# One eviction copy for the column transform, and a filter layer that contracts over 64 rows: a whitening, Fourier filter and MLP kernel on Trainium2

## The chip, the cores and the metric

The kernel runs on one core of one Trainium2 chip. The metric is device microseconds (us) of one execution, the median of the runs shown. TensorE (PE) has two entries in the profile, matrix multiplications (PE) and weight loads (PEld); VectorE is DVE, ScalarE is ACT, GpSimd is POOL, and SyncE (SP) issues the transfers.

## What is computed

The input x holds 16 images of 56 x 56 pixels with 64 channels, in fp32. Cut to what matters here:

```
x  = L^-1 (x - mean) * gamma + beta       # L: Cholesky factor of the 64 x 64 channel covariance
h  = layer_norm(x)
xf = rfft2(h)                             # per image, over rows and columns, 29 x 29 kept parts
o1 = relu(w1 * xf + b1)                   # complex, block diagonal: 8 blocks of 8 x 8 channels
o2 = softshrink(w2 * o1 + b2)             # complex, block diagonal
h  = irfft2(o2) + h + x
out = gelu(layer_norm(h) @ mw1 + mb1) @ mw2 + mb2 + h     # 64 -> 256 -> 64 channels
```

## The kernel before

Two images are one pair: its 2 x 56 image rows stand on 112 partitions, and 56 x 64 numbers in each. There are 8 pairs, numbered 0 to 7 here. A first part reads all pairs once for the covariance and factors it. Then every pair goes through whitening, the filter and the MLP in one software pipeline: in the step of pair i, TensorE runs the filter of pair i, and between its pieces the whitening of pair i + 1 and the MLP of pair i - 1. Each engine's order is written out by hand in its own program; a loop covers the middle pairs, and the first and the last steps are written out. Engines meet only through counting semaphores. SP issues the load of a pair behind the seven stores of an earlier one.

The filter of a pair begins with three stages that go through one ring of four PSUM banks (`ring_b`, lines 246 and 247). A chunk may be written once the chunk four places before it has been read out; `free_b` (line 866) waits for that.

- `dft_h` (line 922): 8 chunks of the row transform. ACT evicts each with one copy of 112 x 464 (line 1121).
- `dft_w` (line 934): 8 chunks of the column transform, 4 matmuls each, 1 in the last. The result of a chunk holds image b in partitions 64b to 64b + 63 (32 channels, real and imaginary part of the row transform) and, in the free dimension, the sum over the cosines (s = 0) and over the sines (s = 1). ACT evicts it into `p_y` with four copies of 64 partitions (line 1133): image b's part s goes to partitions 64s to 64s + 63, so that one matmul of 128 rows adds the cosine and the sine part.
- `layer_1` (line 944): 8 chunks, of 435 columns (four times) and of 406, one matmul of 128 rows each with one of two weight sets `w1s`; chunk k is image k % 2. Their results are evicted with bias and relu in two instructions of 64 partitions each: by ACT (line 1142) for chunks 0 to 3, 5 and 7, and by DVE (line 639) for chunks 4 and 6. These move each image's real and imaginary parts from partitions to where the second layer wants them.

Behind `layer_1` TensorE transposes the first slice of the previous pair's normalised tensor (line 1016) and whitens two chunks (line 918), which need earlier whitening chunks evicted by DVE (line 630). Then the MLP's first matmul (line 1030) waits for that transposed slice `n2T`: ACT writes its high part (line 1166), DVE its low part (line 662). ACT does this behind its layer 1 evictions. DVE does it behind the second layer norm of the previous pair (statistics on line 539, small steps on lines 559 to 567 and 415 to 419, lines 580 and 586), two whitening evictions (line 630) and its layer 1 evictions (line 639).

The tables come in with two transfers among the loads of the first part: `cst` (652 KB) and `prm` (771.5 KB). DVE multiplies the weights with their masks there (line 464).

Of the kernel before, what the change touches and what calls it, by code (L numbers as in the profile page):

```python
# [25 lines left out]
ALU = mybir.AluOpType  # L26
# [93 lines left out]
CONST_COLS = {"f1": 2 * KR, "f2": 4 * KF, "invw": 2 * 224, "invh": ROWS, "mask1": 128, "mask2": 128,  # L120
              "below": C, "minus": C, "ident": 128}
PARAM_COLS = {"w1": 256, "w2": 256, "mw1": HID, "mw2": 2 * 128, "beta": C, "g1": C, "b1": C, "mb2": C,
# [11 lines left out]
def build(nc, x, consts, params, out):  # L134
# [5 lines left out]
    with ExitStack() as ctx:  # L140
        def sb(name, shape, dtype=F32):
            return ctx.enter_context(nc.sbuf_tensor(name, shape, dtype))
# [10 lines left out]
        def pp(name, rows=128):  # L153
            return prm[0:rows, p_at[name][0]:p_at[name][1]]
# [3 lines left out]
        w1s = sb("w1s", [128, 256])  # L158
# [60 lines left out]
        DV_WEIGHTS = 7  # L219
# [32 lines left out]
        p_v = p_y[:, 0:2 * 2 * SPEC].rearrange("p (b h k w) -> p b h k w", b=2, h=2, k=KF)  # L252
# [44 lines left out]
        with nc.Block() as block:  # L297
# [114 lines left out]
            def _(dve):  # L412
# [8 lines left out]
                def covariance_and_factor():  # L421
# [40 lines left out]
                    for t, src, mask in ((w1s, "w1", "mask1"), (w2s, "w2", "mask2")):  # L462
                        for h in range(2):
                            link(nc.vector.tensor_tensor(t[:, 128 * h:128 * h + 128],
                                                         pp(src)[:, 128 * h:128 * h + 128], cc(mask), ALU.mult))
# [343 lines left out]
            def _(pe):  # L809
# [300 lines left out]
            def _(act):  # L1110
# [149 lines left out]
def constants():  # L1260
# [35 lines left out]
    m1 = np.zeros((2, 2, CH, 2, 2, CH))  # L1296
    for cs, r in ((0, 0), (0, 1), (1, 0), (1, 1)):
        for s, sign in enumerate((1.0, -1.0)):
            to_re = (cs == r)
            coef = {(0, 0): 1.0, (1, 1): sign, (0, 1): sign, (1, 0): -1.0}[cs, r]  # L1300
            m1[cs, r, :, s, 0] = same * coef * (1.0 if to_re else -1.0)
            m1[cs, r, :, s, 1] = same * coef
# [13 lines left out]
def layout(i):  # L1316
# [16 lines left out]
    a = np.zeros((2, 2, G, BS, 2, 2, 2, G, BS), np.float32)  # L1333
    for cs in range(2):
        for r in range(2):
            for ro in range(2):
                part = ro if cs == r else 1 - ro
                a[cs, r, :, :, :, :, ro] = w1[part].transpose(1, 2, 0, 3)[:, :, :, None, None, :]
# [39 lines left out]
```

## Time and profile before

| | |
|---|---|
| median of 3 runs | 1033.61 us (1033.3 to 1036.7) |
| the profiled execution | 1037.1 us, of which the span of its instructions 1035.2 us |
| mean granted TensorE clock | 0.927 of full |
| PE busy | 908.7 us, 88% |
| DVE busy | 716.5 us, 69% |
| ACT busy | 557.1 us, 54% |

The profile is one execution. Times in the rows below are us from the start of its span. The column transform starts at 194.1 us for pair 0, and then at 269.2, 369.7, 474.0, 577.3, 679.6, 781.5 and 878.5 us for pairs 1 to 7. Fp32 matmuls stand as two instructions each in the trace, so a count there is twice that of the program.

### The profile page before, as it was taken

What the parts mean: (1) busy time and instruction counts of PE and PEld (TensorE: products, weight loads), DVE (VectorE), ACT (ScalarE), POOL (GpSimd) and SP (SyncE); (2) the same over time, 40 slices, a digit from 0 to 9 for tenths busy, and PEclk for the clock granted to TensorE, in tenths of its full rate; (3) what the DMA queues carried; (4) which work ended last, traced back from release to release, by engine and by line L of the source; (5) the groups of instructions that cost most, each with busy time, mean ns of one, the idle gap of its engine ahead of it and who ended that gap; (6) DMA issues with size and microseconds to landing.
All of it is one profiled execution on the core that took longest, in us unless ns stands there. A gap on an engine that the chain in (4) does not pass through costs nothing.

```text
span 1035.2 us, 18451 instructions
## 1 busy us (share of the span) xinstructions
PE 908.7 (88%) x6263; PEld 775.4 (75%) x6263; DVE 716.5 (69%) x2061; ACT 557.1 (54%) x1139; POOL 261.0 (25%) x107
## 2 busy tenths in 40 slices
PE   5888973887999988998899889988998999799687
PEld 5886552765689768976897689768976997499465
DVE  4356779169957876877677777877788688543762
ACT  0002001674777586757675767586748754875333
POOL 2000001333332234223422342234315324330110
PEclk8995556889999999999999999999999999899789
DMA  9950202002000020002000200110000000000001
GB/s 258 233 125 1 62 1 62 2 1 62 2 10 28 28 63 9 27 19 71 9 27 22 68 11 25 33 57 18 18 27 1 20 27 20 0 28 26 11 28 36
DMA packets 9956, 40.78 MB, mean 39 GB/s; under 512 B 1232, under 2 KB 1232, under 8 KB 8208
## 3 DMA queue, kind: packets, MB, share of 16 engines
q1 hardware_dynamic: 9888, 40.00, 14.3%
q8 instruction: 27, 0.44, 0.2%
q14 instruction: 41, 0.34, 0.1%
HBM read 27.15 MB, written 12.85 MB: 39 GB/s over the span
## 4 chain that ended last, share of the span: by engine, by line
PE 53%; DVE 21%; issue 10%; ACT 9%; DMA 6%; DVEq 0%; SPq 0%; ACTq 0%
PE psum L1045 16%; PE psum L1030 8%; PE psum L983 8%; DMA n<-x_dram 6%; ACT p_y L1133 5%; PE psum L964 4%; DVE stats L539 4%; PE psum L930 3%; ACT o_g L1142 3%; PE psum L918 3%; PE psum L1004 3%; PE psum L857 3%; DVE o_g L294 2%; PE psum L905 2%; PE psum L1016 2%
## 5 line engine op out<-in xcount | busy, mean ns | idle before, releaser
L1174 ACT ACTIVATE hid<-psum,hbias 128x448 f32<-128x448 f32 x224 | 136.1, 633 | 141.4 <-PE psum L1030 140.5
L1045 PEld LDWEIGHTS psum<-prm,hid 128*112 128x112 f32 x1792 | 186.2, 182 | 8.5 <-ACT hid L1174 4.5
L1045 PE MATMUL psum<-prm,hid 128*112 128x96 f32 x1792 | 190.5, 266 | 2.2 <-ACT hid L1174 2.2
L364 POOL TENSOR_TENSOR hbuf<-hbuf,prm 112x1792 f32<-112x1792 f32 x15 | 51.6, 3439 | 337.5 <-DVE hbuf L613 337.5
L662 DVE TENSOR_TENSOR n2T<-psum,n2T 64x448 fp32r<-64x448 f32 x112 | 69.7, 622 | 94.4 <-ACT n2T L1166 93.1
L1030 PE MATMUL psum<-n2T,mw1h 128*128 128x448 f32 x224 | 103.3, 461 | 30.0 <-DVE n2T L662 17.4
L392 POOL TENSOR_TENSOR p_y<-over,under 116x512 f32<-116x512 f32 x64 | 77.5, 1212 | 167.1 <-ACT under L1192 167.0
L983 PE MATMUL psum<-cst,p_y 116*128 116x224 f32 (+1 forms) x480 | 101.8, 355 | 3.0 <-POOL p_y L392 3.0
L983 PEld LDWEIGHTS psum<-cst,p_y 116*128 116x128 f32 (+1 forms) x480 | 89.9, 194 | 6.2 <-POOL p_y L392 3.2
L1133 ACT COPY p_y<-psum 64x232 f32<-64x232 f32 (+1 forms) x256 | 84.3, 329 | 13.9 <-PE psum L940 10.3
L1030 PE MATMUL psum<-n2T,mw1l 128*128 128x448 f32 x224 | 84.1, 376 | 0.0
L1030 PEld LDWEIGHTS psum<-n2T,mw1h 128*128 128x128 f32 x224 | 43.8, 195 | 50.2 <-DVE n2T L662 19.2
L371 POOL TENSOR_TENSOR rbuf<-hbuf,ybuf 112x3584 f32<-112x3584 f32 x8 | 62.7, 7835 | 69.8 <-DVE fbuf L699 63.7
L382 POOL TENSOR_TENSOR fbuf<-fbuf,prm 112x3584 f32<-112x3584 f32 x7 | 54.4, 7773 | 101.1 <-DVE n L586 101.1
L1115 ACT ACTIVATE xT<-psum,negm 128x448 f32<-128x448 f32 x56 | 35.5, 636 | 80.6 <-PE psum L905 80.4
L951 PE MATMUL psum<-p_y,w1s 128*128 128x406 f32 (+1 forms) x128 | 60.7, 563 | 20.2 <-ACT o_g L1142 10.9
L539 DVE BATCH_NORM_STATS2 stats<-fbuf 112x6 f32<-112x64 f32 x448 | 58.5, 210 | 28.2 <-issue 28.2
L1121 ACT COPY u_r<-psum 112x464 f32<-112x464 f32 x64 | 34.9, 546 | 74.8 <-PE psum L930 74.8
L930 PE MATMUL psum<-cst,hbuf 112*112 112x116 f32 x512 | 55.3, 271 | 17.1 <-DVE hbuf L798 17.1
L1166 ACT CAST n2T<-psum 64x448 fp32r<-64x448 f32 x112 | 58.8, 525 | 21.3 <-PE psum L1016 19.6
L930 PEld LDWEIGHTS psum<-cst,hbuf 112*112 112x112 f32 x512 | 55.0, 185 | 20.3 <-issue 20.0
L680 DVE TENSOR_TENSOR oslice<-psum,fbuf 112x512 f32<-112x512 f32 x56 | 38.5, 687 | 45.5 <-PE psum L1045 44.5
(114 smaller groups left out, 1714.2 us busy)
## 6 DMA issues: line engine op xcount, KB each, us to landing
xin<-x_dram SPq DMA_DIRECT2D x9, 1568.0 KB, 8.6
out_dram<-oslice SPq DMA_DIRECT2D x56, 224.0 KB, 2.2
ybuf<-x_dram SPq DMA_DIRECT2D x2, 1568.0 KB, 21.5
fbuf<-x_dram SPq DMA_DIRECT2D x2, 1568.0 KB, 25.1
n<-x_dram SPq DMA_DIRECT2D x2, 1568.0 KB, 28.5
xin<-x_dram SPq DMA_DIRECT2D x4, 392.0 KB, 6.0
prm<-params_dram SPq DMA_DIRECT2D x1, 771.5 KB, 29.7
cst<-consts_dram SPq DMA_DIRECT2D x1, 652.0 KB, 21.1
```

Of the source, the lines that this page charges most:

```text
L371: nc.gpsimd.tensor_tensor(r4, h_tok, y4, ALU.add).then_inc(r_ready, 1)
L392: nc.gpsimd.tensor_tensor(yk, a, b, ALU.subtract).then_inc(y_ready, 1)
L539: last = nc.vector.bn_stats(stats[:, w, :], src[:, w * C:(w + 1) * C])
L662: last = nc.vector.tensor_tensor(n2T[C * (1 - v):C * (1 - v) + C, v, :], ring_c[k % RING_C][C * v:C * v + C, 0:4 * ROWS], n2T[C * v:C * v ...
L930: last = nc.tensor.matmul(t[0:ROWS, j * 2 * KR:(j + 1) * 2 * KR], h_w[:, 4 * k + j, :], cc("f1", ROWS), start=True, stop=True)
L951: nc.tensor.matmul(t[:, 0:(z - a) * KF], w1s[:, 128 * half:128 * half + 128], p_v[:, b, half, a:z, :].rearrange("p k w -> p (k w)"), start ...
L983: last = nc.tensor.matmul(t[:, j * 224:j * 224 + n * 112], y_v[0:n * KR, kp, 128 * r:128 * r + 128], inverse(r, n), start=(r == 0), stop=( ...
L1030: last = nc.tensor.matmul(t[:, 0:4 * ROWS], wt[:, HH * m:HH * m + HH], n2T[:, v, :], start=(p == 0), stop=(p == 1))
L1045: last = nc.tensor.matmul(t[0:ROWS, at:at + 96], hid[:, m, w % 2, (w // 2) * ROWS:(w // 2 + 1) * ROWS], pp("mw2")[:, 128 * m + zeros:128 * ...
L1133: last = nc.scalar.copy(p_v[C * s:C * s + C, b, :, 4 * k:4 * k + n, :], t[C * b:C * b + C, s])
L1166: nc.scalar.copy(n2T[C * v:C * v + C, v, :], ring_c[k % RING_C][C * v:C * v + C, 0:4 * ROWS]).then_inc(hi_ready, 1)
L1174: nc.scalar.activation(hid[:, q % 2, q // 2, :], ring_c[k % RING_C][:, 0:4 * ROWS], ACT.Gelu, bias=hbias[:, q % 2:q % 2 + 1]).then_inc(c_a ...
```

## The change

The column transform's chunk is evicted with one copy of all 128 partitions; each image stays on its own 64 partitions, and s becomes a free dimension of `p_y`. The first filter layer cannot add cosine and sine parts over 128 rows any more: each chunk is now two matmuls of 64 rows that accumulate (s = 0, then s = 1), image 0 on rows 0 to 63 and image 1 on rows 64 to 127. The chunks of two images are taken together: TensorE waits until both banks are free, then issues s = 0 for image 0 and image 1, then s = 1 for both. `w1s` has four blocks of 128 columns in place of two, with the same numbers in both halves of the partitions; its table in `prm` and its mask in `cst` double, and DVE makes two more products in the first part.

```diff
-CONST_COLS = {... "mask1": 128, ...}
+CONST_COLS = {... "mask1": 256, ...}
-PARAM_COLS = {"w1": 256, ...}
+PARAM_COLS = {"w1": 512, ...}
...
-        DV_WEIGHTS = 7
+        DV_WEIGHTS = 9
...
-        p_v = p_y[:, 0:2 * 2 * SPEC].rearrange("p (b h k w) -> p b h k w", b=2, h=2, k=KF)
+        p_v = p_y[:, 0:2 * 2 * SPEC].rearrange("p (s h k w) -> p s h k w", s=2, h=2, k=KF)
...
                 def layer_1(i):
-                    for k in range(8):
-                        part, half, b = k // 4, k // 2 % 2, k % 2
+                    for k in range(0, 8, 2):
+                        part, half = k // 4, k // 2 % 2
                         pe.wait_ge(b_act, i * B_ACT + b_done("act", S2 + 3 if part == 0 else L1 - 1))
-                        t = free_b(i, L1 + k)
                         a, z = L1_PARTS[part]
-                        nc.tensor.matmul(t[:, 0:(z - a) * KF], w1s[:, 128 * half:128 * half + 128],
-                                         p_v[:, b, half, a:z, :].rearrange("p k w -> p (k w)"),
-                                         start=True, stop=True).then_inc(pe_b, 1)
+                        t = [free_b(i, L1 + k + b) for b in range(2)]
+                        for s in range(2):
+                            for b in range(2):
+                                one = nc.tensor.matmul(t[b][:, 0:(z - a) * KF],
+                                                       w1s[C * b:C * b + C, 256 * s + 128 * half:256 * s + 128 * half + 128],
+                                                       p_v[C * b:C * b + C, s, half, a:z, :].rearrange("p k w -> p (k w)"),
+                                                       start=(s == 0), stop=(s == 1))
+                                if s == 1:
+                                    one.then_inc(pe_b, 1)
...
-                        t = ring_b[k % RING_B][:, 0:n * 4 * KF].rearrange("p (k s h w) -> p s h k w", s=2, h=2, w=KF)
-                        for b in range(2):
-                            for s in range(2):
-
-                                last = nc.scalar.copy(p_v[C * s:C * s + C, b, :, 4 * k:4 * k + n, :],
-                                                      t[C * b:C * b + C, s])
-                        last.then_inc(b_act, 1)
+                        t = ring_b[k % RING_B][:, 0:n * 4 * KF].rearrange("p (k m w) -> p m k w", m=4, w=KF)
+                        nc.scalar.copy(p_v[:, :, :, 4 * k:4 * k + n, :].rearrange("p s h k w -> p (s h) k w"), t).then_inc(b_act, 1)
```

On TensorE, in the step of pair 0, the rows from the last chunk of the column transform (line 940) over one whitening chunk (line 918) to the first layer (line 951) and the next whitening stand like this before:

```order
216 L940 MATMUL psum<-cst,u_r 128x116 [waits b_act]
217 L918 MATMUL psum<-wy,xT 112x128 [waits a_act]
218 L918 MATMUL psum<-wy,xT 112x128 x3
219 L951 MATMUL psum<-p_y,w1s 128x435 [waits b_act] x4
220 L951 MATMUL psum<-p_y,w1s 128x406 [waits b_act] x4
221 L918 MATMUL psum<-wy,xT 112x128 [waits a_dve,a_act]
```

And of the changed kernel, where the same three places have lines 944, 922 and 957:

```order
216 L944 MATMUL psum<-cst,u_r 128x116 [waits b_act]
217 L922 MATMUL psum<-wy,xT 112x128 [waits a_act]
218 L922 MATMUL psum<-wy,xT 112x128 x3
219 L957 MATMUL psum<-p_y,w1s 128x435 [waits b_act]
220 L957 MATMUL psum<-p_y,w1s 128x435 x3
221 L957 MATMUL psum<-p_y,w1s 128x435 [waits b_act]
222 L957 MATMUL psum<-p_y,w1s 128x435 x3
223 L957 MATMUL psum<-p_y,w1s 128x406 [waits b_act]
224 L957 MATMUL psum<-p_y,w1s 128x406 x3
225 L957 MATMUL psum<-p_y,w1s 128x406 [waits b_act]
226 L957 MATMUL psum<-p_y,w1s 128x406 x3
227 L922 MATMUL psum<-wy,xT 112x128 [waits a_dve,a_act]
```

Eight matmuls with a wait each have become sixteen with one wait for every four; nothing else changed places.

On ACT, in the same step, from the row transform's copies (line 1121) over those of the column transform (line 1133), before:

```order
4 L1121 COPY u_r<-psum 112x116x4 [waits pe_b] x8
5 L1133 COPY p_y<-psum 64x2x116 [waits pe_b]
6 L1133 COPY p_y<-psum 64x2x116 x3
7 L1133 COPY p_y<-psum 64x2x116 [waits pe_b]
8 L1133 COPY p_y<-psum 64x2x116 x3
```

And of the changed kernel, up to the first layer's evictions (now line 1146):

```order
4 L1130 COPY u_r<-psum 112x116x4 [waits pe_b] x8
5 L1139 COPY p_y<-psum 128x4x116 [waits pe_b] x7
6 L1139 COPY p_y<-psum 128x4x29 [waits pe_b]
7 L1146 ACTIVATE o_g<-psum,prm 64x15x29 [waits pe_b]
8 L1146 ACTIVATE o_g<-psum,prm 64x15x29
```

Thirty-two copies of half the partitions have become eight of all; the order around them is the same.

## Rows read from the trace of the kernel before

**Rows 1.** Timeline, ACT, pair 1: start us, us, engine, line, operation, count, idle before.
```profile
270.42 10.99 ACT L1133 COPY p_y<-psum 64x232 f32<-64x232 f32 x32 [1.31 <-PE psum L940]
281.43 7.62 ACT L1142 ACTIVATE o_g<-psum,prm 64x435 f32<-64x435 f32 x12
289.08 1.08 ACT L1166 CAST n2T<-psum 64x448 fp32r<-64x448 f32 x2
```

**Rows 2.** Timeline, PE, pair 1.
```profile
269.24 6.71 PE L940 MATMUL psum<-cst,u_r 112*128 112x116 f32 x56
276.25 0.48 PE L940 MATMUL psum<-cst,u_r 112*128 112x116 f32 x2 [0.30 <-ACT p_y L1133]
277.70 1.00 PE L951 MATMUL psum<-p_y,w1s 128*128 128x435 f32 x2
...
291.04 0.46 PE L1030 MATMUL psum<-n2T,mw1h 128*128 128x448 f32 x1 [1.32 <-DVE n2T L662]
```

**Rows 3.** Timeline, DVE, pair 1.
```profile
289.64 1.26 DVE L662 TENSOR_TENSOR n2T<-psum,n2T 64x448 fp32r<-64x448 f32 x2 [2.02 <-ACT n2T L1166]
```

**Rows 4.** Timeline, DVE, pair 4.
```profile
577.90 6.30 DVE L539 BATCH_NORM_STATS2 stats<-fbuf 112x6 f32<-112x64 f32 x49 [6.67 <-issue]
...
595.73 1.28 DVE L630 TENSOR_TENSOR ybuf<-psum,prm 112x512 f32<-112x512 f32 x2
596.93 2.61 DVE L639 TENSOR_SCALAR o_g<-psum,prm 64x406 f32<-64x406 f32 x4
599.57 1.26 DVE L662 TENSOR_TENSOR n2T<-psum,n2T 64x448 fp32r<-64x448 f32 x2
```

**Rows 5.** Timeline, ACT and PE, pair 4.
```profile
597.11 1.08 ACT L1166 CAST n2T<-psum 64x448 fp32r<-64x448 f32 x2
...
596.47 2.00 PE L918 MATMUL psum<-wy,xT 128*112 128x128 f32 x16 [0.48 <-DVE ybuf L630]
600.97 0.47 PE L1030 MATMUL psum<-n2T,mw1h 128*128 128x448 f32 x1 [2.49 <-DVE n2T L662]
```

**Rows 6.** Groups by line and shape: busy us, mean ns, idle before, releaser.
```profile
L1121 ACT COPY u_r<-psum 112x464 f32<-112x464 f32 x64 | 34.9, 546 | 74.8 <-PE psum L930 74.8
```

**Rows 7.** Timeline, PE: eight 448-column instructions; four of 58 rows.
```profile
567.02 3.19 PE L1004 MATMUL psum<-o_g,cst 122*112 122x448 f32 x8
...
545.09 0.70 PE L983 MATMUL psum<-cst,p_y 58*128 58x112 f32 x4
```

**Rows 8.** Timeline, DVE, first part.
```profile
64.97 3.89 DVE L438 TENSOR_TENSOR rbuf<-n,pilot 112x3584 f32<-112x3584 f32 x1 [3.78 <-DMA n<-x_dram]
...
75.56 0.23 DVE L472 COPY gtmp<-psum 64x66 f32<-64x66 f32 x1 [4.34 <-PE psum L822]
```

**Rows 9.** Stretches: busy of PE, PEld, DVE, ACT, POOL, clock, DMA share, GB/s.
```profile
20.00:65.00 45.00, 40.19 (x313) 39.81 (x314) 19.50 (x6) 0.00 (x0) 0.00 (x0) 0.89 1.02 238
...
394.00:398.00 4.00, 4.00 (x17) 3.45 (x17) 1.62 (x3) 1.58 (x3) 2.46 (x1) 0.59 0.00 0
...
497.00:500.00 3.00, 2.64 (x11) 2.49 (x12) 1.52 (x3) 0.63 (x1) 3.00 (x1) 0.52 0.00 0
...
601.00:604.00 3.00, 3.00 (x20) 2.59 (x21) 1.84 (x3) 1.46 (x3) 2.70 (x1) 1.00 0.00 0
...
900.00:904.00 4.00, 3.76 (x9) 2.25 (x10) 0.18 (x1) 1.92 (x4) 0.00 (x0) 0.50 0.00 0
```

**Rows 10.** Timeline, PE: MLP starts of pairs 2 and 3, row transforms of 3, 4, 5.
```profile
393.74 0.46 PE L1030 MATMUL psum<-n2T,mw1h 128*128 128x448 f32 x1 [2.49 <-DVE n2T L662]
...
466.78 3.44 PE L930 MATMUL psum<-cst,hbuf 112*112 112x116 f32 x33
...
497.36 0.73 PE L1030 MATMUL psum<-n2T,mw1h 128*128 128x448 f32 x1 [2.49 <-DVE n2T L662]
...
570.04 6.51 PE L930 MATMUL psum<-cst,hbuf 112*112 112x116 f32 x64
...
672.37 6.51 PE L930 MATMUL psum<-cst,hbuf 112*112 112x116 f32 x64
```

More of the change, by code:

```diff
@@ L117, in c_reader @@
     return "dve", out_done(s)
-CONST_COLS = {"f1": 2 * KR, "f2": 4 * KF, "invw": 2 * 224, "invh": ROWS, "mask1": 128, "mask2": 128,
+CONST_COLS = {"f1": 2 * KR, "f2": 4 * KF, "invw": 2 * 224, "invh": ROWS, "mask1": 256, "mask2": 128,
               "below": C, "minus": C, "ident": 128}
-PARAM_COLS = {"w1": 256, "w2": 256, "mw1": HID, "mw2": 2 * 128, "beta": C, "g1": C, "b1": C, "mb2": C,
+PARAM_COLS = {"w1": 512, "w2": 256, "mw1": HID, "mw2": 2 * 128, "beta": C, "g1": C, "b1": C, "mb2": C,
               "fb2": 256, "gamma": 1, "g2": 1, "b2": 1, "fb1": 2, "mb1": 2}
@@ L157, in build @@
         wy = sb("wy", [128, 128])
-        w1s = sb("w1s", [128, 256])
+        w1s = sb("w1s", [128, 512])
         w2s = sb("w2s", [128, 256])
@@ L461, in covariance_and_factor @@
                     dve.wait_ge(s_prm, 16)
-                    for t, src, mask in ((w1s, "w1", "mask1"), (w2s, "w2", "mask2")):
+                    for s in range(2):
                         for h in range(2):
-                            link(nc.vector.tensor_tensor(t[:, 128 * h:128 * h + 128],
-                                                         pp(src)[:, 128 * h:128 * h + 128], cc(mask), ALU.mult))
+                            cols = slice(256 * s + 128 * h, 256 * s + 128 * h + 128)
+                            link(nc.vector.tensor_tensor(w1s[:, cols], pp("w1")[:, cols],
+                                                         cc("mask1")[:, 128 * s:128 * s + 128], ALU.mult))
+                    for h in range(2):
+                        link(nc.vector.tensor_tensor(w2s[:, 128 * h:128 * h + 128],
+                                                     pp("w2")[:, 128 * h:128 * h + 128], cc("mask2"), ALU.mult))
                     link(nc.vector.tensor_scalar(mw1s[:], pp("mw1"), pp("g2"), None, ALU.mult))
@@ L944, in layer_1 @@
                 def layer_1(i):
-                    for k in range(8):
-                        part, half, b = k // 4, k // 2 % 2, k % 2
+                    for k in range(0, 8, 2):
+                        part, half = k // 4, k // 2 % 2
                         pe.wait_ge(b_act, i * B_ACT + b_done("act", S2 + 3 if part == 0 else L1 - 1))
-                        t = free_b(i, L1 + k)
                         a, z = L1_PARTS[part]
-                        nc.tensor.matmul(t[:, 0:(z - a) * KF], w1s[:, 128 * half:128 * half + 128],
-                                         p_v[:, b, half, a:z, :].rearrange("p k w -> p (k w)"),
-                                         start=True, stop=True).then_inc(pe_b, 1)
+                        t = [free_b(i, L1 + k + b) for b in range(2)]
+                        for s in range(2):
+                            for b in range(2):
[5 more added lines that the diff above has]
+                                    one.then_inc(pe_b, 1)
                 def layer_2(i, half, k):
@@ L1295, in constants @@
     same = np.kron(np.eye(CH // BS), np.ones((BS, BS)))
-    m1 = np.zeros((2, 2, CH, 2, 2, CH))
+    m1 = np.zeros((2, 2, CH, 2, 2, 2, CH))
     for cs, r in ((0, 0), (0, 1), (1, 0), (1, 1)):
@@ L1300, in constants @@
             coef = {(0, 0): 1.0, (1, 1): sign, (0, 1): sign, (1, 0): -1.0}[cs, r]
-            m1[cs, r, :, s, 0] = same * coef * (1.0 if to_re else -1.0)
-            m1[cs, r, :, s, 1] = same * coef
+            m1[:, r, :, cs, s, 0] = same * coef * (1.0 if to_re else -1.0)
+            m1[:, r, :, cs, s, 1] = same * coef
     put("mask1", m1.reshape(128, -1))
@@ L1332, in layout @@
     w2 = i["L1_conv_w2"].reshape(2, 2, G, BS, BS)
-    a = np.zeros((2, 2, G, BS, 2, 2, 2, G, BS), np.float32)
+    a = np.zeros((2, 2, G, BS, 2, 2, 2, 2, G, BS), np.float32)
     for cs in range(2):
@@ L1337, in layout @@
                 part = ro if cs == r else 1 - ro
-                a[cs, r, :, :, :, :, ro] = w1[part].transpose(1, 2, 0, 3)[:, :, :, None, None, :]
+                a[:, r, :, :, cs, :, :, ro] = w1[part].transpose(1, 2, 0, 3)[None, :, :, :, None, None, :]
     put("w1", a.reshape(128, -1))
```

## The prediction, made before the changed kernel was run

> **What bounds the kernel now.** I first asked where TensorE stands still, since it is busy 88% of the span. In the steady part it does so almost only between the column transform and the MLP's first matmul. The timeline of pair 1 shows why. ACT is the late engine: its 32 half-width copies run without a gap for 10.99 us, its twelve layer 1 evictions follow for 7.62 us, and only then does it write n2T at 289.08 us [rows 1]. DVE waits 2.02 us for that [rows 3], and TensorE's MLP starts at 291.04 us, 21.8 us behind the start of the column transform [rows 2]. TensorE itself needs only 6.7 us for the column transform and is then slowed by banks that ACT has not read [rows 2].
>
> The same stretch of pair 4 reads otherwise, and that is the main point of this forecast. TensorE waits 2.49 us at the same matmul [rows 5], but ACT began n2T at 597.11 us [rows 5] and DVE took it up only at 599.57 us, without any wait: DVE ran from 577.90 us on through the second layer norm, two whitening evictions and four layer 1 evictions, one behind the other [rows 4]. It had started late: it stood 6.67 us for "issue" at its loop's end, waiting for nothing that the profile names [rows 4]. DVE's first reason to wait for ACT there is the first half of n2T, ready 0.54 us behind 597.11, so ACT was 1.9 us early. Pair 2 is alike (TensorE waits the same 2.49 us for DVE [rows 10]), and so are 3 and 5. Pairs 0, 1, 6 and 7 are the ones in which ACT is late: there the loop's stall is absent or short. Four pairs of eight can gain.
>
> **The change, part by part.** *The copy.* A chunk's four copies take 1.37 us (10.99 us over 8 chunks, the last a quarter as wide) [rows 1]. The nearest row for one copy of 128 x 464 is the row transform's, 112 x 464 in 546 ns [rows 6]; the other end is that nothing is saved, 1.37 us. I take 0.55 us, since it has the same count in the free dimension, source and destination. With some 0.2 us from a matmul's end to ACT's start that is 0.8 us a chunk, less than TensorE's 0.94 us (8 instructions at 6.71 / 56, less the last one's latency: 0.117 us each) [rows 2]. So TensorE sets the pace; the 0.30 us wait before the last chunk goes [rows 2], the last matmul starts at 275.8 and the whitening chunk behind it (8 x 0.11 us) is through at 276.9 us. ACT has the last copy done by then, so that layer 1 starts at about 277.0 us rather than at 277.70 [rows 2], 0.1 us of which I charge for the change to 64 rows: four 58-row instructions spaced by 0.14 us where 116 columns of 112 rows take 0.117 are the nearest row [rows 7, 2].
>
> *The layer.* An instruction of 448 columns takes (3.19 - 0.55) / 7 = 0.377 us in a stream [rows 7], one of 435 then T = 0.366 us; the two of a chunk before fit this (1.00 us with 0.11 us of weight load ahead and the latency behind) [rows 2]. Two chunks took 4 T. Now they are 8 instructions. No row of this trace shows two matmuls on different rows of the array next to each other, so I bound it: 8 T = 2.9 us if they take turns, and about 5 T = 1.8 us for a lone group if the two images' instructions run beside each other (the two instructions of one image stay one behind the other). I take the second, because rows 0 to 63 and 64 to 127 share no operand and no bank, and keep the first as a rival.
>
> The Trainium skill bears on that. "TensorE: Matmul & The Clock Gate", Part 3, tells of matmuls on different row tiles that run concurrently, and measured 3.07 times the speed for four tiles of 32 rows, which no row here shows. "TensorEngine Tiling (Array Packing)", Key Properties, speaks against: a change of tiling mode drains the engine. Here the 58-row row bounds what a change costs at some 0.1 us [rows 7], and without the sum's 0.1 us each gaining pair would gain that much more.
>
> *ACT behind it.* Layer 1's first result is out at 277.0 + 0.11 + 4 T + 0.17 = 278.7, ACT starts at 278.95. One chunk costs it 7.62 / 6 = 1.27 us [rows 1]. Chunks 0 to 3 end at 284.0. The last two chunks, 6 and 7, may now be written only once chunk 3 is read (before, 6 was let in by 2 alone); both are out by 284.1 + 0.11 + 5 x 0.34 + 0.17 = 286.1, and ACT's eviction of 7 runs 286.3 to 287.5. Before, ACT was through at 289.05 [rows 1]. **Gain: 1.5 us in a pair where ACT is late**, although 49 us of ACT's busy time go (8 x 8 x 0.77): most of it turns into waits for the pairs of banks. DVE's two layer 1 chunks end by about 287.1 and don't take over; TensorE's whitening behind layer 1 ends near 288, and the MLP could start at 289.5. Four pairs: -6.0 us. The four with DVE late: 0, because ACT's 1.9 us of slack only grow. What cover fails there: if ACT were over 1.9 us later than now, it would set the end.
>
> *The first part.* The tables grow by 384 columns of 128 x 4 bytes, 197 KB. The loads of x bind there (DVE waits 3.78 us for the last one) [rows 8], at 238 GB/s in this stretch [rows 9]: +0.8 us. DVE's two more products, some 0.3 us each, lie in its 4.34 us wait for TensorE [rows 8]: 0, and 0.6 if that cover were gone.
>
> *The clock.* Right behind the 2.49 us waits TensorE ran at half its 2.4 GHz for a while in pairs 2 and 3 (granted 0.59 and 0.52 of full), and at full in pair 4 [rows 9]. From the MLP's start to the next row transform it then took 466.78 - 393.74 = 73.04 and 570.04 - 497.36 = 72.68 us, against 672.37 - 600.97 = 71.40 us in pair 4 [rows 10, 5]: such a drop costs 1.3 to 1.6 us. Under the change TensorE comes to this wait in pairs 2 to 5 some 2 us earlier, and stands before the whitening (held at 596.47 us by DVE [rows 5]) for about 2 us too where it stood 0.48. I expect drops in all four pairs, two more than now: +2.9 us.
>
> **Sum:** -6.0 + 0.8 + 2.9 = -2.3 us on a profiled 1037.1 us (span 1035.2). That execution stands 3.5 us over the median of 1033.61; the same difference off the median gives 1031.3 us. About 0.3% (3.1 us) is what a measurement of this kernel can tell from no change.
>
> **The rivals.** *No further drops of the clock*: pairs 4 and 5 stay at full, as now. For it: their waits are those of pairs 2 and 3 to 0.01 us, yet the clock held. -5.2 us, 1028.4 us. Against it: more idling just ahead of the wait.
>
> *The row parts take turns* (the slower side). Place: layer 1 of pairs 0, 1, 6, 7. A group of two chunks takes 2.9 us. By the same chain ACT gets chunk 0 at 279.7, chunks 0 to 3 end at 285.0, TensorE starts the last group at 285.6 and ends it at 288.5, ACT is through at 289.9: 0.85 us later than now. Four pairs +3.4, first part +0.8: +4.2 us, 1037.8 us; the clock as now. Between 1.8 us (-1.5) and 2.9 us (+0.85) a group, the sign of a gaining pair turns near 2.5 us. In the DVE-bound pairs it stays hidden (layer 1 ends 0.6 us later than now on TensorE, against 1.9 us of slack). This would be "does not do what it says" on TensorE. For it: no row shows the contrary.
>
> *Longer drops.* In pair 7 the clock stood at 0.50 from 900 to 904 us behind a wait of 3.0 us [rows 9], and work that starts there at half speed for 6.8 us loses 3.4 rather than 1.4. Were all four DVE-bound pairs like it: 4 x 3.4 - 2.9 = +10.7, with -5.2: +5.5 us, 1039.1 us.
>
> *The copy is no faster than the four.* Then ACT stays late at the start too, and only the coarser waits remain: about +2 us, 1035.6 us. Against it stands the 546 ns of [rows 6]; 5%.
>
> **How the numbers follow.** Forecast as summed 0.38; no further drops 0.22; turns 0.22; longer drops 0.13; slow copy 0.05. The predicted time is that of the forecast, 1031.3 us. The forecast's own spread is 1029.5 to 1033. Leaving out one in ten on either side of all: 1027.5 to 1038.5 us. Faster by over 0.3% (under 1030.5): all of the second case and a fifth of the first, 0.30. Slower (over 1036.7): most of the turns and of the longer drops, 0.30. Same: 0.40.
>
> **What will show it.** The new copy's mean at 0.55 us, and TensorE's column transform without a wait. In layer 1, a group of four matmuls from its first start to its last end: near 2.0 us if side by side, 3.1 us if in turns. The MLP of pair 1 starting 20.3 us behind its column transform (now 21.8), and of pair 4 still 23.7 us behind. DVE's 6 to 7 us of "issue" unchanged in pairs 2 to 5; if ACT's shorter or TensorE's longer program moves that stall, every DVE-bound pair moves with it, and the forecast is wrong by up to 4 x that. The granted clock behind the waits of pairs 2 to 5 decides between the first and second case.

## The result, and the profile after

The changed kernel ran at 1021.18 us (median of 17, 1016.96 to 1029.91), beside the kernel before at 1031.06 (17 runs, 1024.94 to 1036.7) on the same chip: a ratio of 0.9915, 95% interval 0.9889 to 0.9941, or 8.8 us (the two medians stand 9.9 us apart). I had forecast a gain of 2.3 us. The kernel is faster beyond the 0.3% bound, a case to which I had given 0.30, and its time lies below the range that I gave. Of the 10.1 us between my 1031.3 us and the 1021.18, 2.6 come from the kernel before, which measured 1031.06 us here and not 1033.61. The span of its profiled execution is 1022.9 us (before 1035.2), the mean granted clock 0.919.

Lines have moved: the column transform is now 944, its copy 1139, layer 1 957, its evictions 1146 (ACT) and 643 (DVE), n2T 1170 and 666, the MLP's first matmul 1039, the second layer norm 543, whitening 922 and 634. From the page of the changed kernel the busy time of the engines in us, and then groups of instructions by line and shape (busy us, mean ns | idle before, releaser):

```profile
PE 899.1 (88%) x6391; PEld 780.4 (76%) x6391; DVE 717.3 (70%) x2063; ACT 505.4 (49%) x947; POOL 261.5 (26%) x107
```

```profile
L1139 ACT COPY p_y<-psum 128x464 f32<-128x464 f32 x56 | 30.7, 548 | 26.8 <-PE psum L944 26.8
L957 PE MATMUL psum<-p_y,w1s 64*128 64x406 f32 x128 | 26.2, 525 | 17.3 <-ACT o_g L1146 17.3
L957 PE MATMUL psum<-p_y,w1s 64*128 64x435 f32 x128 | 25.5, 537 | 0.0
```

The copy takes 548 ns; ACT's busy time fell by 51.7 us. TensorE issues twice as many layer 1 instructions in less busy time than before: 51.7 us where the two shapes had 60.6. Timeline of pair 1, ACT, PE and DVE (the column transform starts at 264.22 us; before [rows 1 to 3]):

```profile
270.76 0.71 ACT L1139 COPY p_y<-psum 128x464 f32<-128x464 f32 x2 [0.35 <-PE psum L944]
273.52 6.39 ACT L1146 ACTIVATE o_g<-psum,prm 64x435 f32<-64x435 f32 x10 [2.05 <-PE psum L957]
280.42 1.22 ACT L1146 ACTIVATE o_g<-psum,prm 64x406 f32<-64x406 f32 x2 [0.52 <-PE psum L957]
281.66 1.08 ACT L1170 CAST n2T<-psum 64x448 fp32r<-64x448 f32 x2
```

```profile
264.22 6.73 PE L944 MATMUL psum<-cst,u_r 112*128 112x116 f32 x58
270.79 1.04 PE L922 MATMUL psum<-wy,xT 128*112 128x128 f32 x8
271.75 3.19 PE L957 MATMUL psum<-p_y,w1s 64*128 64x435 f32 x16
276.13 1.63 PE L957 MATMUL psum<-p_y,w1s 64*128 64x406 f32 x8 [1.19 <-ACT o_g L1146]
278.72 1.63 PE L957 MATMUL psum<-p_y,w1s 64*128 64x406 f32 x8 [0.95 <-ACT o_g L1146]
...
283.62 0.46 PE L1039 MATMUL psum<-n2T,mw1h 128*128 128x448 f32 x1 [0.98 <-DVE n2T L666]
```

```profile
282.22 1.26 DVE L666 TENSOR_TENSOR n2T<-psum,n2T 64x448 fp32r<-64x448 f32 x2 [0.55 <-ACT n2T L1170]
```

The column transform no longer waits for banks. ACT waits for TensorE in its place, 2.05 us ahead of layer 1's first result. Two groups of four matmuls each (16 instructions) take 3.19 us, and the second group starts 1.57 us behind the first: the two images of a group run side by side all the way. The MLP starts 19.40 us behind the column transform where it had been 21.80. Pair 4, DVE, ACT and PE (column transform at 569.35; before [rows 4, 5]):

```profile
570.33 6.31 DVE L543 BATCH_NORM_STATS2 stats<-fbuf 112x6 f32<-112x64 f32 x49 [7.01 <-issue]
...
592.00 1.26 DVE L666 TENSOR_TENSOR n2T<-psum,n2T 64x448 fp32r<-64x448 f32 x2
```

```profile
586.78 1.08 ACT L1170 CAST n2T<-psum 64x448 fp32r<-64x448 f32 x2
```

```profile
588.90 3.76 PE L922 MATMUL psum<-wy,xT 128*112 128x128 f32 x16 [2.89 <-DVE ybuf L634]
593.39 0.74 PE L1039 MATMUL psum<-n2T,mw1h 128*128 128x448 f32 x1 [0.73 <-DVE n2T L666]
```

Here nothing was won: DVE took its full path behind a 7.01 us stall, ACT began its half of n2T 5.2 us ahead of DVE's, and TensorE's idling only moved, from the MLP's matmul to the whitening ahead of it.

### The profile page after: what moved, and what is told of

It reads as the page before. It is cut to its first block, busy times and chain, and to the rows that moved or that the text cites. A ratio compares the mean times of both kernels' runs of the same rounds, so it can differ in the third digit from the quotient of the medians.

```text
span 1022.9 us, 18505 instructions
## 1 busy us (share of the span) xinstructions
PE 899.1 (88%) x6391; PEld 780.4 (76%) x6391; DVE 717.3 (70%) x2063; ACT 505.4 (49%) x947; POOL 261.5 (26%) x107
## 4 chain that ended last, share of the span: by engine, by line
PE 55%; DVE 24%; issue 10%; DMA 5%; ACT 4%; DVEq 0%; SPq 0%; ACTq 0%
PE psum L1054 15%; PE psum L1039 8%; PE psum L992 8%; DMA n<-x_dram 5%; DVE stats L543 5%; PE psum L973 4%; PE psum L922 3%; PE psum L861 3%; PE psum L934 3%; PE psum L944 3%; PE psum L1013 3%; DVE o_g L294 2%; ACT o_g L1146 2%; PE psum L909 2%; DVE n L584 2%
## 5 line engine op out<-in xcount | busy, mean ns | idle before, releaser
L1054 PEld LDWEIGHTS psum<-prm,hid 128*112 128x112 f32 x1792 | 184.1, 180 | 8.5 <-ACT hid L1178 4.7
L1054 PE MATMUL psum<-prm,hid 128*112 128x96 f32 x1792 | 188.4, 264 | 2.2 <-ACT hid L1178 2.2
L922 PE MATMUL psum<-wy,xT 128*112 128x128 f32 x448 | 66.9, 303 | 13.7 <-DVE ybuf L634 13.0
L922 PEld LDWEIGHTS psum<-wy,xT 128*112 128x112 f32 x448 | 61.3, 201 | 18.8 <-DVE ybuf L634 15.4
L1146 ACT ACTIVATE o_g<-psum,prm 64x435 f32<-64x435 f32 (+1 forms) x96 | 59.4, 619 | 21.3 <-PE psum L957 19.8
L934 PEld LDWEIGHTS psum<-cst,hbuf 112*112 112x112 f32 x512 | 54.5, 184 | 19.8 <-issue 19.8
L934 PE MATMUL psum<-cst,hbuf 112*112 112x116 f32 x512 | 54.7, 270 | 16.7 <-DVE hbuf L802 16.7
```

The lines of the kernel that those rows point to most:

```text
L922: last = nc.tensor.matmul(t[0:ROWS, j * 128:(j + 1) * 128], xT[:, w * ROWS:(w + 1) * ROWS], wy[:], start=True, stop=True)
L934: last = nc.tensor.matmul(t[0:ROWS, j * 2 * KR:(j + 1) * 2 * KR], h_w[:, 4 * k + j, :], cc("f1", ROWS), start=True, stop=True)
L1054: last = nc.tensor.matmul(t[0:ROWS, at:at + 96], hid[:, m, w % 2, (w // 2) * ROWS:(w // 2 + 1) * ROWS], pp("mw2")[:, 128 * m + zeros:128 * ...
L1146: last = nc.scalar.activation(dst, src, ACT.Relu, bias=bias)
```

## The experiments

Every kernel below was run beside the kernel before, and its ratio is to that kernel. This table is worked out from the timelines. It gives the us from a pair's first column transform instruction to the MLP's first matmul.

| pair | before | changed | again | copy only | layer only | load moved, before | load moved, changed |
|---|---|---|---|---|---|---|---|
| 1 | 21.80 | 19.40 | 19.39 | 19.10 | 20.56 | 21.83 | 19.39 |
| 2 | 24.04 | 23.59 | 23.41 | 23.69 | 23.70 | 21.83 | 19.38 |
| 3 | 23.36 | 23.40 | 23.75 | 23.40 | 23.32 | 21.82 | 19.38 |
| 4 | 23.70 | 24.04 | 23.50 | 24.24 | 24.15 | 21.83 | 19.39 |
| 5 | 23.21 | 24.13 | 23.12 | 23.48 | 23.77 | 21.84 | 19.40 |
| 6 | 21.64 | 19.31 | 19.29 | 18.94 | 20.46 | 21.67 | 19.30 |
| 7 | 21.78 | 18.57 | 18.56 | 17.27 | 20.61 | 21.82 | 18.57 |

**The copy alone.** Only the last hunk of the change, on ACT, with the old order of `p_y`'s axes:

```diff
-                        t = ring_b[k % RING_B][:, 0:n * 4 * KF].rearrange("p (k s h w) -> p s h k w", s=2, h=2, w=KF)
-                        for b in range(2):
-                            for s in range(2):
...
-                                last = nc.scalar.copy(p_v[C * s:C * s + C, b, :, 4 * k:4 * k + n, :],
-                                                      t[C * b:C * b + C, s])
-                        last.then_inc(b_act, 1)
+                        t = ring_b[k % RING_B][:, 0:n * 4 * KF].rearrange("p (k m w) -> p m k w", m=4, w=KF)
+                        nc.scalar.copy(p_v[:, :, :, 4 * k:4 * k + n, :].rearrange("p b h k w -> p (b h) k w"), t).then_inc(b_act, 1)
```

> Half of the change: the one copy of 128 partitions, with layer 1 left as before (one matmul of 128 rows a chunk). The cosine and sine parts then don't lie where the layer adds them, so this kernel leaves the right sum out; sizes and counts are those of the kernel before. Theory (the copy gives the whole gain, the layer takes a little back): in pairs 1 and 6 the layer starts 7.5 us behind the column transform, ACT reaches n2T 16.7 us behind it (19.8 before, 17.4 in the changed kernel) and the MLP starts 18.7 us behind it (21.8 before, 19.4 changed); four such pairs, with the two further drops of the clock, give -10 us against the kernel before, some 2 us below the changed kernel. Rival (the side-by-side layer saves time of its own): the MLP starts no earlier than in the changed kernel, 19.4 us or more, and the kernel is at -8 us or less gain. In both, TensorE's clock drops in all four pairs 2 to 5.

Measured: 1014.67 us, ratio 0.9857 (0.9829 to 0.9886), 14.7 us below before. ACT reached n2T 16.0 us behind the column transform (19.8 before, 17.4 changed), better than the 16.7 that I expected, and DVE became the last one in all pairs, so the MLP started at 19.10 and not at 18.7. The theory holds: the copy is the gain, and the 64-row layer gives part of it back, 1.4 us a pair at ACT, but only 0.3 us at the MLP, and 1.3 us in pair 7. Its sizes were off: I had expected 10 us and some 2 us below the changed kernel, and by the ratios it is 6 us below it. Pair 0 has a part in that (71.33 us from its column transform to the next, against 74.28 and 73.30 in the two profiles of the changed kernel). The clock dropped in pairs 2 to 5, as expected, but ahead of the MLP, where it cost nothing, and in pairs 1 and 6 as well.

**The layer alone.** The 64-row matmuls with `p_y` in the new layout, filled by four copies that each keep their image's partitions:

```diff
-                                last = nc.scalar.copy(p_v[C * s:C * s + C, b, :, 4 * k:4 * k + n, :],
+                                last = nc.scalar.copy(p_v[C * b:C * b + C, s, :, 4 * k:4 * k + n, :],
```

> The other half: layer 1 as in the changed kernel (64 rows, two images side by side, one wait for two banks, larger tables), but four copies of 64 partitions for a chunk of the column transform. Theory: ACT's copies take 11 us again, the layer's first result comes 0.5 us later than before and ACT is let in to the last two chunks later, so the MLP of pairs 1 and 6 starts 22.3 to 23.0 us behind the column transform (21.8 before) and the kernel is 2 to 5 us slower than before; pairs 2 to 5 as before, clock drops in two of them only. Rival (the side-by-side layer saves time of its own): below 21.8 us and a gain.

Measured: 1026.61 us, ratio 0.9962 (0.9941 to 0.9982); the MLP at 20.56 us. My theory was wrong in sign: a small gain. It isn't the matmuls. Timeline of ACT in pair 1 (column transform at 265.01), against [rows 1]:

```profile
266.19 9.25 ACT L1141 COPY p_y<-psum 64x232 f32<-64x232 f32 x32 [1.31 <-PE psum L944]
275.46 6.39 ACT L1150 ACTIVATE o_g<-psum,prm 64x435 f32<-64x435 f32 x10
```

The same 32 copies take 9.25 us, not 10.99. By line and shape, before and here:

```profile
L1133 ACT COPY p_y<-psum 64x232 f32<-64x232 f32 x224 | 77.9, 348 | 13.4 <-PE psum L940 10.3
```

```profile
L1141 ACT COPY p_y<-psum 64x232 f32<-64x232 f32 x224 | 66.9, 348 | 12.1 <-PE psum L944 10.3
```

One copy takes 348 ns in both, but 224 of them fill 77.9 us there and 66.9 here: they overlap. By their start times, the second copy of an image starts 0.249 us behind the first, and the next image's 0.357 behind that; before, each starts 0.36 us behind the one ahead. So ACT won 1.74 us on the copies, and the layer took 0.5 us back (from the end of the last copy to n2T 8.17 us, before 7.67).

**Another order of the four copies.** Which of the two partition ranges has to stay?

```diff
-                        for b in range(2):
-                            for s in range(2):
+                        for s in range(2):
+                            for b in range(2):
```

> The kernel before with the four half copies of a chunk in another order: first both images' cosine parts (which go to partitions 0 to 63), then both sine parts (to 64 to 127), so that two consecutive copies write the same partitions but read different ones. With the layer changed alone, ACT's 32 copies took 9.25 us where 10.99 had been: the copies of 0.348 us followed each other by 0.249 us when both read and wrote the same partitions as the one ahead, and by 0.36 us otherwise. Theory A (the same destination partitions are enough): 9.3 us again, ACT reaches n2T 18.1 us behind the column transform (19.8 before), four pairs gain 1.7 us: -5 to -7 us. Theory B (source and destination must both stay): 11.0 us and no change of the time.

Measured: 1029.18 us, ratio 1.0001 (0.9974 to 1.0028), 77.8 us busy for the 224 copies, ACT at n2T after 19.83 us: theory B. Writing the same partitions isn't enough. Nor is reading the same ones: in the kernel before, the two copies of an image read the same partitions and write different ones, and start 0.36 us apart. Both have to stay. Every copy that overlapped also wrote to the partitions that it read from; whether that is needed too isn't told apart.

**Both images on the same rows.** The price of the rival "row parts take turns":

```diff
-   w1s[C * b:C * b + C, ...], p_v[C * b:C * b + C, s, half, a:z, :]
+   w1s[0:C, ...], p_v[0:C, s, half, a:z, :]
```

> The changed kernel with both images' layer 1 matmuls on rows 0 to 63: image 1's chunks then take the numbers of image 0, and those of image 1 are left out; order, sizes and waits stay. It sets the price of the case that I gave 22%, row parts that take turns. Theory: the four matmuls of a group then take 8 T = 2.9 us instead of 1.5, ACT reaches n2T 20 to 21 us behind the column transform and the MLP of pairs 0, 1, 6 and 7 starts 22 to 23 us behind it (19.4 changed, 21.8 before): 10 to 13 us slower than the changed kernel, and slower than the kernel before. Rival (what makes the group short is only that matmuls of 64 rows cost half, on whatever rows): 1.5 us a group and the time of the changed kernel.

Measured: 1030.27 us, ratio 1.0000 (0.9976 to 1.0024). Timeline of PE in pair 1 (column transform at 263.23):

```profile
270.76 11.56 PE L957 MATMUL psum<-p_y,w1s 64*128 64x435 f32 x32
```

32 instructions stand one behind the other at 0.34 to 0.37 us each, 2.9 us a group, with no wait in between: it is the use of both row halves that lets the two images run side by side. The MLP of pair 1 started at 22.32 us and that of pair 7 at 21.44, below the 22 that I expected. The time came out at that of the kernel before, some 9 us above the changed one, and not slower than before as I expected; the rival of the prediction had +4.2 us. What the rival says of a group is what this kernel does, but its 3.4 us for the four pairs measured 1.6 (0.5 in pairs 1 and 6, -0.3 in pair 7, 0.9 in pair 0), and this profile has one drop of the clock fewer than that of before.

**Layer 1 in image order.** Image 0's two matmuls, then image 1's, each chunk behind its own bank:

```diff
-                        t = [free_b(i, L1 + k + b) for b in range(2)]
-                        for s in range(2):
-                            for b in range(2):
+                        for b in range(2):
+                            t = free_b(i, L1 + k + b)
+                            for s in range(2):
...
```

> The changed kernel with layer 1's matmuls in image order (image 0: s = 0, s = 1; then image 1: s = 0, s = 1), each chunk waiting for its own bank alone; everything else as changed. T is one instruction of 435 columns (0.366 us), two of them a matmul. Theory (the two row parts of the array work independently, so that image 1's first matmul runs beside image 0's second): the first chunk is out after 4 T as now, the next ones every 2 T; ACT, let in by single banks, evicts without a gap (12 in 7.6 us) and reaches n2T 16.9 us behind the column transform (17.4 in the changed kernel); the MLP starts 19.1 us behind it (DVE binds then), 0.3 us less in pairs 1 and 6 and 1 us less in pair 7: -2 us against the changed kernel. Rival (side by side only in the order s = 0 of both, then s = 1 of both): a chunk takes 4 T, 1.46 us, for itself, all eight over 11 us, ACT reaches n2T at 20.6 us, the MLP starts at 22.6 us, and the kernel is 10 to 13 us slower than the changed one.

Measured: 1022.54 us, ratio 0.9933 (0.9907 to 0.9960), the same as the changed kernel. The rival is out, but my theory's detail was wrong too, and the 2 us that I expected on top didn't come. In the first group the start times are 0.00, 0.01, 0.47, 0.48, 0.83, 0.85, 1.20, 1.21 us, as in the changed kernel: eight instructions run in pairs though four of one image are queued ahead of four of the other. Since two on the same rows never start together (the run above), each pair must be one of each image. The semaphores in the trace agree: the weight load beside the second start, at 0.01 us, carries a wait for a bank, which stands only ahead of an image's first matmul, and both instructions of the fourth pair signal ACT, which only the last one of an image does. So TensorE doesn't keep the queue's order between row parts. In the second group the two images soon run 0.11 us apart. The last four chunks, each behind a bank of its own, run singly. ACT reached n2T at 17.38 us (changed 17.44).

**The load moved away from the loop's end.** DVE's stall [rows 4] stands beside SP's load of x for a later pair. The load was issued at 569.04 us and had landed 9.1 us later, 0.25 us behind DVE's restart at 577.90. From 569 to 575 us the DMA engines moved only that load and the end of the store ahead of it, and no instructions. The DMA queues between 575 and 577 us, and then from 577 to 579 (packets, MB, share of the 16 engines' time):

```profile
q1 hardware_dynamic: 32, 0.26, 50.1%
q14 instruction: 1, 0.01, 1.4%
```

```profile
q1 hardware_dynamic: 3, 0.01, 1.8%
q14 instruction: 1, 0.01, 1.6%
```

Packets of instructions (queue 14) arrive only as the load ends. The edit on SP (the load for i = 3 stands ahead of the loop):

```diff
-                with sp.Fori(1, PAIRS - 2) as i:
-                    sp.wait_ge(pe_a, (i + 1) * A_CHUNKS + 7)
-                    load(i + 2)
-                    for s in range(SLICES):
-                        store(i - 1, s)
+                with sp.Fori(1, PAIRS - 3) as i:
+                    for s in range(4):
+                        store(i - 1, s)
+                    sp.wait_ge(pe_a, (i + 2) * A_CHUNKS + 7)
+                    load(i + 3)
+                    for s in range(4, SLICES):
+                        store(i - 1, s)
...
```

> The kernel before with one thing moved: the load of x for a later pair is issued behind the fourth store of a step in place of ahead of the first, so that it doesn't stand beside the ends of the engines' loop steps. Theory (DVE's 6 to 7 us of 'issue' at the loop's end is its next instructions being fetched behind the 1.6 MB load in the same DMA engines): the stall falls to about 2 us, as in pair 6 where no load runs; the four DVE-bound pairs then become bound by ACT, 1.9 us earlier each: -7 us against before. Rival (the stall belongs to the loop's jump itself, or to something else that DVE waits for there): it stays 6 to 7 us and the time within 1 us of before. The load is needed only a whole step later, so that its later issue costs nothing.

> The changed kernel with the same move of the load. Theory: DVE's stall falls from 6.4 to 7.1 us to about 2 us, pairs 2 to 5 become ACT-bound, and there ACT is 4 us earlier in this kernel, so the MLP starts 19.4 us behind the column transform (23.4 to 24.1 now): -4 us each, -16 us against the changed kernel, and some -25 us against the kernel before; that is more than twice what the move brings in the kernel before, and shows how much of the change's gain the stall hides. The clock's drops should stay. Rival (the stall is not the load's): within 1 us of the changed kernel.

Measured: 1018.05 us, ratio 0.9894 (0.9866 to 0.9922), for the kernel before; 1000.35 us, ratio 0.9712 (0.9686 to 0.9738), for the changed one. DVE's restart in pair 4 of the first, and its n2T and TensorE's MLP in pair 4 of the second:

```profile
563.42 2.76 DVE L543 BATCH_NORM_STATS2 stats<-fbuf 112x6 f32<-112x64 f32 x21 [2.09 <-issue]
```

```profile
573.74 1.26 DVE L670 TENSOR_TENSOR n2T<-psum,n2T 64x448 fp32r<-64x448 f32 x2 [0.38 <-ACT n2T L1174]
...
575.13 0.46 PE L1043 MATMUL psum<-n2T,mw1h 128*128 128x448 f32 x1 [0.98 <-DVE n2T L670]
```

The stall fell to 2.0 to 2.2 us in all four pairs, pairs 2 to 5 became copies of pair 1 (table), and the clock stayed at full beside the MLP starts of pairs 1 to 6, where I had expected its drops to stay. The move alone brought 11 us (I had expected 7), and 21 us on top of the change (16). The change is then worth 17.7 us, 1018.05 to 1000.35, where it brought 8.8: about half of it had been hidden behind that stall. The changed kernel with the moved load is faster than either edit alone.

The packets settle more than the landing does. DVE's first instruction behind its loop's end comes 1.9 to 2.3 us behind the start of an 8 KB packet of instructions in each of the 65 such places of the 13 profiles, worked out from the packets' times. That packet starts 0.1 to 0.4 us behind DVE's stop where no load runs, and 3.8 to 5.0 us behind it where a whole load does. So the stall is this packet's delay, and about 2.1 us.

**Half a load.** Is it the load's length, or its being there? Against the kernel before with the load moved (only the issues inside the loop are shown):

```diff
+                    load(i + 2, hi)
                     for s in range(4):
                         store(i - 1, s)
...
-                    load(i + 3)
+                    load(i + 3, lo)
```

> The kernel before with half of each load of x (784 KB) left at the step's start and the other half behind the fourth store. Theory (DVE's restart waits for the end of the transfer, since its instructions are fetched behind it): the half load lands some 4.5 to 5 us after its issue in place of 9, so that DVE's stall is 2.5 to 3.5 us (2.0 to 2.2 with the load away, 6.2 to 7.0 with all of it), and pairs 2 to 5 are bound by ACT, as with the load away: the time of that kernel, 0.99 of before. Rival (a load at that place costs the stall whatever its size, by its issue or by SP's place in the loop): 6 to 7 us, time as before.

Measured: 1018.05 us, ratio 0.9859 (0.9809 to 0.9909). The stall was 3.5 to 4.3 us, at and above my 2.5 to 3.5 and well below 6, so the load's length counts. Issued at 557.46, the 784 KB took 5.5 us to land in place of the 4.5 to 5 that I took, and DVE went on 1.0 us behind that. With whole loads it went on between 0.9 us ahead of the landing and 0.1 behind it, so the restart does not wait for the landing itself; the packet of instructions came 1.3 to 2.2 us behind DVE's stop here, and the restart 2.0 to 2.2 us behind the packet, as everywhere. With a stall of 2.1 us or of 4.2, ACT is later than DVE, and the MLP starts at 21.8 us either way.

**Image order and the moved load.**

> Both edits together: the load of x moved behind the fourth store, and layer 1 in image order. Theory: all eight pairs wait for ACT then, and MLP starts move from 19.4 to 19.1 us behind the column transform: 2 to 3 us below the kernel with the moved load alone, near 0.969 of the kernel before. Rival (no side-by-side work in this order): 3 us a pair slower, some 1024 us.

Measured: 1000.92 us, ratio 0.9717 (0.9694 to 0.9741), no different from the moved load alone, where I had expected 2 to 3 us less; the MLP started at 19.34 us, 0.05 less. The coarser wait for two banks costs next to nothing.

**The copy alone and the moved load.**

> The one copy with layer 1 as before (the layer's sum is then not the right one, as in the run of the copy alone), and the load moved behind the fourth store. It asks what is left of the copy's gain when neither DVE's stall nor the 64-row layer is there. Theory by waits alone: MLP 19.1 us behind the column transform in all pairs, against 19.4 with the 64-row layer: 2 us below the changed kernel with the moved load, some 998 us. Rival (the clock): with the copy alone, TensorE stood 2.44 us in pairs 1 and 6 ahead of the MLP and the clock dropped there (72.8 us from the MLP to the next row transform in pair 1, not 71.4). With the load away all of pairs 1 to 5 look like pair 1, and each loses 1.4 us: 1003 to 1006 us, slower than the changed kernel with the moved load, though ACT is through 1.4 us earlier in every pair.

Measured: 1000.87 us, ratio 0.9722 (0.9658 to 0.9786), with the clock rival's mechanism in pairs 1 to 5. PE in pair 4, and then two stretches there (busy us of PE, PEld, DVE, ACT and POOL, then the granted clock, as in [rows 9]):

```profile
575.08 0.74 PE L1034 MATMUL psum<-n2T,mw1h 128*128 128x448 f32 x1 [2.49 <-DVE n2T L666]
```

```profile
574.00:578.00 4.00, 2.92 (x11) 2.77 (x12) 2.29 (x5) 0.90 (x2) 3.79 (x1) 0.61 0.00 0
579.00:582.00 3.00, 3.00 (x30) 2.96 (x28) 0.69 (x1) 1.85 (x4) 0.00 (x0) 1.00 0.00 0
```

From the MLP to the next row transform pairs 1 to 5 took 72.6 to 73.0 us, not 71.4. A step took 99.15 us, against 98.04 us in the changed kernel with the moved load: with ACT through 1.4 us earlier, the steady step was 1.1 us longer. The totals came out equal all the same, and the rival's 1003 to 1006 us did not come. In the two profiles five steps cost 5.8 us more here; pair 0 was 2.0 us shorter and pair 7's MLP started 1.3 us earlier, and the other 3.6 us lie ahead of the first column transform and behind pair 7's MLP start, where runs differ by as much without any change. So the longer step is shown, and the equal totals are in part chance.

**The changed kernel again.**

> The changed kernel once more, to have it in one set of runs with the others and to see which of its differences repeat. Theory: 19.4 us from column transform to MLP in pairs 1 and 6, 18.6 in pair 7, and 23.3 to 24.2 us in pairs 2 to 5 (DVE's stall of 6 to 7 us varies from pair to pair and run to run); a drop of the clock beside the MLP wait of pairs 2 and 3 at least; the first 190 us and the time behind pair 7's MLP start differ by up to 3 us from run to run without any change of the kernel. Rival: what the first comparison showed of the first 190 us (4.1 us less) belongs to the change and repeats to within 1 us.

Measured: 1023.28 us, ratio 0.9920 (0.9890 to 0.9950). The MLP starts repeat to 0.02 us in pairs 1, 6 and 7. The first column transform was at 190.95 us, 1.0 us behind the first profile's 189.95. That is the rival's bound, but the five kernels with the old tables other than the one before had it at 186.9 to 190.8 us too, so the runs don't ascribe it to the change.

## Why the prediction was wrong

The steps in order, with both profiles of the changed kernel against the one of before (us, worked out from the timelines and rounded):

| term | forecast | first | again |
|---|---|---|---|
| MLP start, pairs 1, 6, 7 | -4.5 | -7.9 | -8.0 |
| pair 0, column transform to column transform | -1.5 | -0.9 | -1.9 |
| MLP start, pairs 2 to 5 | 0 | +0.9 | -0.5 |
| MLP start to next row transform, pairs 2 to 5 (clock) | +2.9 | +2.0 | -1.4 |
| first 190 us | +0.8 | -4.1 | -3.1 |
| behind pair 7's MLP start | 0 | -2.2 | -2.3 |
| sum | -2.3 | -12.3 | -17.2 |

- **Which pairs gain** was right: pairs 0, 1, 6 and 7, and none of 2 to 5, and for the reason given: DVE behind its stall, with ACT's slack growing from 1.9 to 4.7 us [rows 4, 5].
- **The gain of such a pair** was mis-sized, and this is the step that failed: 1.5 us forecast, 2.4 measured in pairs 1 and 6, and 3.2 in pair 7. I had ACT at n2T 18.26 us behind the column transform; it was 17.44. Half of the difference is the layer's start and first result. The layer began at 7.53 us, not 7.76, since the column transform's 58 instructions took 6.57 us, 0.113 each, where I took 0.117 from a row that held waits for banks. ACT got its first chunk 1.77 us later, not 1.95. Most of the other half is the last group, which I priced at 5 T (T is one instruction's time) because "the two instructions of one image stay one behind the other". They do, but the other image's run fully beside them, so it is 4 T. In pair 7 no whitening chunk stands ahead of layer 1, which began at 6.66 us; that is another 0.8 us that I didn't look for. With this term alone set right the sum would be -6.2 us.
- **The copy** was priced right, 0.55 against 0.548 us, and so was the change to 64 rows: layer 1 starts 0.96 us behind the whitening chunk ahead of it, and 0.87 us with 128 rows behind the new copy. The Trainium skill, "TensorEngine Tiling (Array Packing)", Key Properties, has TensorE drained at a change of mode; if the 0.09 us between these rows are that drain, it is short. No run tells it apart.
- **The first part** shows no cost of the tables. Its last tile of x began at 57.6 to 61.1 us in the seven runs with the larger tables, and at 57.8 to 65.0 us in the six without. The profile of before was the latest of all [rows 8]. That, and not the change, is most of the -4.1 us. What lies behind pair 7's MLP start varies in the same way: 133.1 to 135.0 us in the kernels with the old layer and four copies, 131.7 to 135.4 with the new layer and one copy.
- **The clock.** Drops did come in all four DVE-bound pairs in both profiles, as forecast; the price didn't. Stretches of the changed kernel beside the MLP starts at 385.86, 489.51, 593.39 and 698.29 us:

```profile
386.00:390.00 4.00, 4.00 (x16) 3.44 (x17) 1.74 (x3) 1.38 (x3) 2.56 (x1) 0.59 0.00 0
486.00:492.00 6.00, 4.63 (x22) 4.16 (x20) 4.56 (x8) 0.63 (x1) 6.00 (x1) 0.50 0.00 0
588.00:592.00 4.00, 3.10 (x14) 3.10 (x15) 3.91 (x8) 1.16 (x1) 3.68 (x1) 0.51 0.00 0
594.00:598.00 4.00, 4.00 (x17) 3.76 (x16) 1.27 (x2) 1.53 (x3) 2.09 (x1) 0.50 0.00 0
693.00:697.00 4.00, 3.20 (x15) 3.20 (x16) 3.91 (x8) 0.97 (x1) 3.78 (x1) 0.62 0.00 0
```

  TensorE idles ahead of the whitening now (2.89 us in pair 4), so the drop tends to begin there. Where it is all but over before the MLP starts, as in pair 5 (693 to 697), TensorE only waits for DVE more slowly, and nothing is lost; that was so in pairs 2 to 4 of the second profile. I had priced every drop at 1.3 to 1.6 us from [rows 9, 10], where it began at the MLP's matmul. So this term failed too: +2.9 us forecast, +2.0 and -1.4 in the two profiles.

Between the two profiles the terms that belong to the steady part sum to -5.9 and -11.8 us, on either side of the 8.8 us measured. With 2.4, 2.4, 3.2 and 1.9 us for the four pairs (pair 0 from the second profile; the first has 0.9), 9.9 us, and the first part and the clock near nothing, my own sum would have come within about 1 us of it. That the clock's term is near nothing on average isn't shown: two profiles differ by 3.4 us in it. The chances failed with it: I put the range's lower end at 1027.5 us by spreading over what could go wrong, and nowhere asked what a side-by-side run in full would give.

## What to carry to other kernels

Group the pairs or steps by which engine is late before pricing a change; here only half of them could gain, and the other half hid as much again behind one stall. An "issue" wait at a loop's end is worth a look at what the DMA engines carry just then: moving one load brought about as much as the change by itself, 11 against 9 us, and doubled what the change is worth. And where an engine's share of a side-by-side run isn't known, carry the best case as a rival too, not only the worst.

## What the runs showed of the hardware

- Two fp32 matmuls on rows 0 to 63 and 64 to 127 run at the speed of one: 16 instructions in 3.19 us, starting 6 to 7 ns apart, where the same on one row half take 6.1 us. The Trainium skill, "TensorE: Matmul & The Clock Gate", The mechanism, has matmuls start and end strictly in program order; the starts and semaphores of the run in image order speak against that between row parts.
- Consecutive ACT copies of 64 x 232 overlapped by 0.1 us where they read and wrote the same partitions as the one ahead, and not where either changed (0.249 against 0.36 us from start to start, at 0.348 us each). The Trainium skill, "ScalarE: Activation LUTs", What ACT_TABLE_LOAD costs, gives about 93 ns for the overlap of ACTIVATE instructions back to back; for these copies the trace agrees in size, and shows a condition.
- An ACT copy from PSUM of 128 x 464 took 548 ns, one of 128 x 116 took 262 and one of 64 x 232 took 348. A line through the first two gives an estimate of 357 ns for 128 x 232, so half the partitions save next to nothing, and the free count sets the time.
- At its loop's end DVE stood 6.0 to 7.2 us beside a 1568 KB load, 3.5 to 4.3 beside half of it, and 2.0 to 2.3 beside none. In all of these places it went on 1.9 to 2.3 us behind the start of a packet of instructions, and it was this packet that came late beside a load.
- What a drop of the clock cost depended on what TensorE had to do during it: between 0 and 2.1 us a pair, with nothing lost where it fell into a wait for DVE.
